# A graph network's attention layers: each group of edge rows stored by two strided DMAs in place of one contiguous DMA

## The reference, cut to what matters

```python
h = (x @ W).reshape(n, heads, -1)
al_s = jnp.einsum('nhf,hf->nh', h, a_src)
al_d = jnp.einsum('nhf,hf->nh', h, a_dst)
e = jax.nn.leaky_relu(al_s[src] + al_d[dst], NEG_SLOPE)
m = jax.lax.stop_gradient(jax.ops.segment_max(e, dst, num_segments=n))
ex = jnp.exp(e - m[dst])
denom = jax.ops.segment_sum(ex, dst, num_segments=n)
alpha = ex / (denom[dst] + 1e-16)
out = jax.ops.segment_sum(h[src] * alpha[:, :, None], dst, num_segments=n)
```

## Time and profile before

| what | us |
|---|---|
| median of three runs (lowest, highest) | 6648.58 (6619.81, 6655.24) |
| the profiled execution's own time | 6668.59 |
| its span, first to last instruction | 6666.8 |
| DVE busy, share of the span | 4655.7, 70% |
| POOL busy, share of the span | 3990.8, 60% |
| ACT busy, share of the span | 3180.9, 48% |
| PE busy, share of the span | 1584.1, 24% |
| attention, layer 1: first to last `z` | 1699.42 to 3887.03 |

### The profile page before, as it was taken

One profiled execution on the slowest core, in us unless ns is written; L12 is line 12 of the kernel. 1 busy time (PEld: TensorE's weight loads), 2 busy tenths in 40 slices (PEclk: granted clock), 3 DMA queues, 4 the chain that ended last, 5 costly groups with the idle time before them and its releaser, 6 DMA issues. The chain is left out here.

```text
span 6666.8 us, 34527 instructions
## 1 busy us (share of the span) xinstructions
PE 1584.1 (24%) x7221; PEld 1283.6 (19%) x7221; DVE 4655.7 (70%) x8059; ACT 3180.9 (48%) x2937; POOL 3990.8 (60%) x3935
## 2 busy tenths in 40 slices
PE   6777799998000000000000015300000000000000
PEld 5665588886000000000000004200000000000000
DVE  7889577776676777666777744477667676666755
ACT  7885122222354555555555533255555555555540
POOL 1430344443766766666766646577777777777756
PEclk8779899999555555555555557655555555555555
DMA  8999433333555565555555535365555555555548
GB/s 319 343 342 350 164 124 121 121 121 110 161 180 187 197 206 186 183 187 195 194 190 202 182 132 134 98 215 186 185 199 186 191 186 186 190 187 198 185 161 305
DMA packets 358517, 1281.85 MB, mean 192 GB/s; under 512 B 83184, under 2 KB 175408, under 8 KB 328272
## 3 DMA queue, kind: packets, MB, share of 16 engines
q1 hardware_dynamic: 167984, 756.10, 30.7%
q0 software_dynamic: 180320, 471.38, 24.5%
q10 hardware_dynamic: 10048, 52.70, 2.0%
HBM read 676.46 MB, written 603.41 MB: 192 GB/s over the span
## 5 line engine op out<-in xcount | busy, mean ns | idle before, releaser
L162 POOL DMA_INDIRECT rows<-table_d,k_src x3128 | 3123.9, 999 | 1257.8 <-issue 1147.7
L217 ACT ACTIVATE rows<-totals 128x1472 f32<-128x1472 f32 x544 | 2088.7, 3863 | 1408.8 <-DVE totals L308 1051.4
L308 DVE TENSOR_TENSOR_SCAN totals<-mask,turned 128x1536 f32<-128x1536 f32 x544 | 1806.4, 3341 | 71.9 <-DMA g1b<-in_g_b 64.2
L180 PE MATMUL pB<-diag,k_ones 128*128 128x512 f32 (+1 forms) x4 | 2.9, 821 | 4410.1 <-DVE diag L327 2227.2
L299 DVE TENSOR_TENSOR turned<-rows,pT 128x1472 f32<-128x1472 f32 x544 | 916.2, 1684 | 0.0
L180 PEld LDWEIGHTS pB<-diag,k_ones 128*128 128x128 f32 x4 | 1.0, 310 | 4410.8 <-DVE diag L327 2227.5
L720 PE MATMUL pH<-hT_pre,w1h 128*128 128x256 f32 x1568 | 463.6, 460 | 120.9 <-ACT hT_pre L598 108.8
L265 DVE TENSOR_TENSOR z<-rows,ad 128x92 f32<-128x92 f32 (+1 forms) x136 | 28.9, 212 | 642.7 <-DMA rows<-table_d,k_src 596.5
L1095 POOL DMA_INDIRECT lone_ea<-in_ea,k_gather x196 | 205.8, 1050 | 442.5 <-DVE mid_feat L1304 368.2
L720 PEld LDWEIGHTS pH<-hT_pre,w1h 128*128 128x128 f32 x1568 | 361.3, 237 | 208.5 <-ACT hT_pre L598 126.8
L1138 PE MATMUL pM<-fT,w1e 128*128 128x256 f32 x1568 | 364.6, 386 | 1.3 <-issue 1.3
(11 more groups left out here) (248 smaller groups left out, 3654.6 us busy)
## 6 DMA issues: line engine op xcount, KB each, us to landing
sums_d<-rows SPq DMA_DIRECT2D x68, 3036.0 KB
sums_d<-rows SPq DMA_DIRECT2D x68, 2967.0 KB
ea<-in_ea SPq DMA_DIRECT2D x98, 768.0 KB
rows_d<-run SPq DMA_DIRECT2D x97, 768.0 KB
pre_d<-pre ACTq DMA_DIRECT2D x49, 1024.0 KB
pre_in<-pre_d SPq DMA_DIRECT2D x49, 1024.0 KB
rows<-table_d,k_src POOLq DMA_INDIRECT x3128
hrow_c<-table_d SPq DMA_DIRECT2D x98, 256.0 KB
```

Of the source, the lines that this page charges most:

```text
L162: p.indirect_dma_start(out=rows[:, g.slot, k, :], out_offset=None, in_=table, in_offset=bass.IndirectOffsetOnAxis(ap=keep["src"][:, e:e + ...
L217: a.activation(rows[:, g.slot, :, q * PD:(q + 1) * PD], totals[:, q, :, 1:].rearrange("p d k -> p k d"), ACT.Copy).then_inc(rowed, 1)
L308: v.tensor_tensor_scan(totals[:, q, :, :].rearrange("p d k -> p (d k)"), mask[:, g.n % 2, :, :].rearrange("p d k -> p (d k)"), turned[q % ...
```

## The change

The view `outv` keeps rows and features apart, and the store of a group becomes two DMAs on SP: the first takes the group's rows 0, 2, ..., 22 (12 of them), the second rows 1, 3, ..., 21 (11). Since every second row is skipped, a piece that is contiguous on both sides is one row, 1056 or 1032 bytes. A group is then 2944 pieces in place of 128, of the same bytes in all. Each of the two DMAs adds 16 to `stored`, so the waits count in 32s.

```diff
-        outv = rows_out.rearrange("(p e) f -> p (e f)", p=P)
+        outv = rows_out.rearrange("(p e) f -> p e f", p=P)
...
             for g in groups:
                 sp.wait_ge(rowed, PARTS * (g.n + 1))
-                sp.dma_start(outv[:, g.first * W:g.end * W],
-                             rows[:, g.slot, :, :].rearrange("p k w -> p (k w)")).then_inc(stored[g.slot], 16)
+                for k in range(2):
+                    sp.dma_start(outv[:, g.first + k:g.end:2, :], rows[:, g.slot, k::2, :]).then_inc(stored[g.slot], 16)
...
-                    p.wait_ge(stored[g.slot], 16 * g.use)
+                    p.wait_ge(stored[g.slot], 32 * g.use)
...
-                p.wait_ge(stored[i], 16 * len(groups[i::SLOTS]))
+                p.wait_ge(stored[i], 32 * len(groups[i::SLOTS]))
```

## The result

The changed kernel takes 6681.41 us (median of 20 runs, 6635.89 to 6697.03) and the kernel before, beside it, 6636.57 (20 runs). The ratio is 1.0054 with a 95% interval of 1.0038 to 1.0071: 36 us more, 25 to 47. (The means lie 35.3 us apart. The medians lie 44.8 apart, since the runs of each kernel fall into two clusters some 34 us apart, which the two kernels share out differently.) The forecast was 79 us more. The direction was right, the size about twice too large.

A forecast was written before the change was run, and what follows sets the result against it. It took POOL's issue to bound layer 2 and, in layer 1, a rhythm of long and short groups set by POOL's lead, cause unknown. Layer 1's 74 plus 5 at the ends gave +79, 6728 us on the median's scale; range 6440 to 6860.

The forecast's parts named there:

- The second DMA on SP: Store issue on SP: 136 more issues of 0.32 us and a hold of about 10 us, hidden, so nothing.
- The store's length: Each group's store: one-row pieces move at 307 GB/s, 10.1 us in place of 7.8, so 2.3 us longer.
- the bound of 5.3 from above: Store's length: upper bound on its growth, 2.3 us plus 3 us for gathers passing between the pieces.
- The release comes later and layer 1 pays for it: Layer 1: POOL's waits that begin a group end 2.3 us later, lead smaller by 0.08; 74 us more.
- one short group less in each cycle: Layer 1: five groups in 168.3 us, 33.7 a group in place of 32.5, 74 us more; chance 0.34.
- a lead of about 1.27: Layer 1: groups POOL's issue stands ahead of DVE's; at 1.27 a group was long, at 1.30 short.
- cycle of six: Layer 1 before the change: three long groups, then three short, 194.9 us a cycle, 32.5 a group.
- Layer 2: 0: Layer 2: POOL sets the pace and waits for no store, so 0; ends open at +57 and -204 us.
- `z` even, no alternate waits of 15 us: Sign for layer 2: `z` starts evenly, without alternate 15 us waits, still at 1.40 us a gather.
- The ends: 5: Each layer's end: the last store lies bare before `fix`, 2 x 2.3 = 5 us more.
- The faster rival: Attention layers: gathers land on time and the rhythm relaxes; layer 2 alone -204 us, both -437; chance of faster 0.33.
- 272 us by a serial fixed part: Stores: 136 more DMAs, each with a fixed part of some 2 us, would add 272 us if serial.

The follow-up runs named there:

- the late release: Kernel before, its stores unchanged, but POOL released by a small DMA that SP issues once the store has landed; ratio 1.0073, in the repeat 1.0059.
- four slots: Kernel before with SLOTS = 4 in place of 3; ratio 1.0027, layer 1 2208.3 us.
- the execution without the limit: Store as two DMAs of contiguous 12 and 11 rows, run again, without the pace of about 1.40 us a gather; 6123.7 us against 6148.57 before, ratio 0.9992.
- Two contiguous halves: Changed kernel with each group's store as two DMAs of contiguous 12 and 11 rows; ratio to the kernel before 1.0034, again 0.9992.

## Why the prediction was right or wrong

- **The second DMA on SP: nothing.** Right in effect. But the hold was put at 10 us and measured 0.8 to 1.4. The earlier trace rows was a poor guide: a second DMA of 1024 KB had been issued 1.05 us before the one that was counted.
- **The store's length: 2.3 us more.** Right in layer 1, 9.9 to 12.1 us, and there the pace of the earlier trace rows held. In part that was luck: layer 2's store, whose pieces are 1032 bytes, grew from 9.8 to 15.8 us, beyond the bound of 5.3 from above. It cost nothing but at the end, since nobody waits for it, as said.
- **The release comes later and layer 1 pays for it.** Right, and shown by the late release, which has this of the change and none of its pieces. That nothing else of the change costs is not shown.
- **"Between 0.9 and 3.1 us of longer store it is one short group less in each cycle: five groups in 194.9 - 26.6 = 168.3 us", 74 us.** This step failed. The three short groups stayed; a cycle has seven groups in place of the five forecast, with one more that is partly long, and costs 0.4 us a group more, not 1.2. Layer 1 lost 26.7 us (27, 29 and 20 in three profiles). Behind it stands the assumption that a long group begins below a lead of about 1.27. In the changed kernel a short group starts at a lead of 1.24 (2654.63, POOL back at 2619.07) and the first long one at 1.17, with four slots it starts at 2.24. The rows had a better key: 65 us from POOL's last break. The working also took its cycle of six for the rhythm, where the trace begins with two of seven. And it put the wait before `carried_w` down to DVE's own increments, where the row names ACT; of the 581 us the profile ends some 97 by ACT's exponentials, so it isn't DVE's increments alone that come late. Had I kept a balance in place of an edge, a pace of 1.40 that loses whatever time POOL's break leaves it without work, I'd have found that the count of before is empty once in each of 10 cycles, for some 2 us. By this estimate, made after the result, a release 2.3 us later adds that at this break, and up to as much at the break before it: 23 to 46 us.
- **Layer 2: 0.** The sum was right. "`z` even, no alternate waits of 15 us" was wrong: the waits are 11 and 5 us here, 568.5 us in all against 587.6. Gathers still starve beside small pieces: in the first 6 us from a store's issue the median is 88 of their packets in layer 1 and 86 in layer 2, against 74 and 80 beside large ones. The 63 of the earlier trace rows are of a stretch that begins 0.4 us after the issue; from the issue on it is 76.
- **The ends: 5.** Near: 2.0 and 4.9 us more from the last store's issue to `fix`, 6.9 in all. Outside the two layers as a whole it can't be seen (641.3 us against 645.3).
- **The faster rival** rested on the slower pace being a state and not a need. That was right, and its 204 us for layer 2 is what the execution without the limit gave (2134.5 to 1931.2). But the store's pieces aren't what sets the state. The rule of the Trainium skill behind it, "DMA: Bandwidth & Descriptors", Queues, rings and completion order, has DMA engines go round the queues packet by packet. That gathers would keep most of their rate beside one-row pieces, the traces don't bear out: 88 packets against 74 in layer 1, of some 225 that they'd move alone in 6 us.
- **272 us by a serial fixed part**, from the same page's Anatomy of one DMA, which gives that figure for DMAs that GpSimd issues, while the stores are SP's. Two contiguous halves took 10.2 us from issue to last packet against 9.9 for one DMA. So whatever fixed part the second DMA has lies, but for 0.3 us, beside the first's transfer.

## What to carry to other kernels

When a stage has a pace that no engine's busy time explains, keep a balance over it before you build on a threshold: who feeds it, at what rate it drains, and when it stands empty. What a longer transfer costs is then to be sought in what its later end takes from that pace, and a small delayed release is a cheap experiment to show it, since it leaves the transfer alone. And before a per cent is explained, look whether the whole rhythm is the kernel's: here the same programs also ran without it, in some 500 us less.

## What the runs showed of the hardware

- A gather of 128 rows was issued every 1.25 us, but in all profiles but one only one in 1.40 us went through for long. The signs were DVE's waits on its own and on ACT's increments (581 us in layer 1) or POOL's steps of 1.401 (layer 2), and semaphore updates that are late or missing in the trace (5,421 against 29,221 of one program's layer 1). What fills is not named by any view. The DMA engines weren't full: before the change 24.2% and 32.2% of their time went to stores and gathers in layer 1. In the execution without the limit gathers ran at their full pace beside stores of the same bytes, cut in two.
- Piece size on a store of 3.1 MB, issue to last packet, layer 1: 9.9 us in pieces of 24,288 bytes, 10.2 in 11 to 13 KB, 12.1 in 1056 bytes, 16.5 in 528. At 1032 bytes (layer 2) 15.8, in one DMA 20.0, and 26 at 516 bytes. The step from 1056 to 1032 bytes is larger than the size explains, and no run shows why.
- A DMA of 128 pieces of 4 bytes behind a store, with the limit there, let POOL go on 6.9 us after its issue (median over the layer's waits 7.2).
